# Two-layer GRU and mixture of experts on one core: at which slots of a chunk layer 1 makes all its gates in one PSUM bank

## The reference, cut to what matters

```python
def step(h, xt):
    hg = h @ Whh.T + bhh
    xr, xz, xn = jnp.split(xt, 3, axis=-1)
    hr, hz, hn = jnp.split(hg, 3, axis=-1)
    r = jax.nn.sigmoid(xr + hr)
    z = jax.nn.sigmoid(xz + hz)
    n = jnp.tanh(xn + r * hn)
    h_new = (1.0 - z) * n + z * h
...
h1 = _gru_layer(mixed, Wih0, Whh0, bih0, bhh0)
h2 = _gru_layer(h1, Wih1, Whh1, bih1, bhh1)
...
x = x + gated_output(h2)       # and then
x = x + mixture_of_experts(x)
```

## Time and profile before

| what | value |
|---|---|
| median of 3 runs | 2167.6 us (2160.2 to 2175.3) |
| the profiled execution's own time | 2176.5 us |
| its span, first to last instruction | 2174.5 us |
| slots, of which the last 19 hold layer 1 alone | 1043 |
| PE, DVE, ACT busy | 95%, 84%, 52% |

### The profile page before, as it was taken

How to read it: one execution, slowest core, us unless ns; L and a number is a source line. 1 busy time by engine, 2 the same in 40 slices (tenths; PEclk the granted TensorE clock), 3 DMA queues, 4 the chain that set the end, 5 groups by cost and what they waited for, 6 DMA issues and landing times.

```text
span 2174.5 us, 162405 instructions
## 1 busy us (share of the span) xinstructions
PE 2061.9 (95%) x70040; PEld 1501.8 (69%) x70040; DVE 1818.0 (84%) x11343; ACT 1141.1 (52%) x6471; POOL 560.3 (26%) x2542
## 2 busy tenths in 40 slices
PE   6999999999999999999999999999999999999997
PEld 4666667777677776777667776777767776777765
DVE  3788888888888888888888888888888888888885
ACT  2555555555555555555555555555555555555542
POOL 1222232222322223222232222222232222222220
PEclk9999999999999999999999999999999999999999
DMA  5000000000000000000000000000000000000000
GB/s 220 5 5 5 4 5 5 5 5 5 10 5 5 5 5 10 5 5 5 10 5 5 5 5 10 5 5 5 5 10 5 5 5 10 5 5 9 5 5 9
DMA packets 7184, 24.32 MB, mean 11 GB/s; under 512 B 1584, under 2 KB 3904, under 8 KB 6208
## 3 DMA queue, kind: packets, MB, share of 16 engines
q1 hardware_dynamic: 6464, 13.93, 1.7%
HBM read 11.83 MB, written 2.10 MB: 6 GB/s over the span
## 4 chain that ended last, share of the span: by engine, by line
PE 61%; DVE 25%; ACT 10%; issue 3%; DMA 0%; SPq 0%; POOL 0%; POOLq 0%; DVEq 0%
PE bank L335 28%; PE bank L327 18%; PE bank L267 11%; DVE bank L406 8%; DVE cells L426 7%; ACT factors L476 6%; DVE z_pre L407 5%; DVE r_pre L397 4%; ACT cells L480 4%; PE bank L308 3%; DVE bank L415 1%; PE bank L274 0%; DMA x_t<-in_x_t 0%; DVE x L682 0%; DVE n_second L382 0%
## 5 line engine op out<-in xcount | busy, mean ns | idle before, releaser
L335 PE MATMUL bank<-w_h,cells 128*22 128x128 f32 (+4 forms) x32768 | 1377.8, 281 | 22.8 <-DVE cells L426 11.9
L335 PEld LDWEIGHTS bank<-w_h,cells 128*22 128x22 f32 (+4 forms) x32768 | 865.7, 111 | 129.5 <-DVE cells L426 81.1
L327 PEld LDWEIGHTS bank<-w_h,cells 128*2 128x2 f32 (+15 forms) x28112 | 527.2, 113 | 493.8 <-DVE cells L426 464.8
L521 POOL TENSOR_SCALAR cells<-cells 128x4 f32<-128x4 f32 x2048 | 463.7, 226 | 1516.8 <-DVE cells L426 1515.1
L327 PE MATMUL bank<-w_h,cells 128*2 128x64 f32 (+15 forms) x28112 | 782.5, 225 | 72.8 <-DVE cells L426 54.0
L470 ACT ACTIVATE n_second<-r_pre 128x4 f32<-128x4 f32 x2048 | 426.5, 208 | 516.1 <-DVE r_pre L397 477.3
L476 ACT ACTIVATE factors<-z_pre 128x4 f32<-128x4 f32 x2048 | 429.5, 210 | 478.7 <-DVE z_pre L407 427.6
L426 DVE TENSOR_TENSOR_SCAN cells<-factors,cells 128x18 f32<-128x18 f32 x2048 | 396.5, 194 | 227.2 <-ACT cells L480 154.2
L406 DVE STREAM_TRANSPOSE bank<-bank 128x64 f32<-128x64 f32 x2048 | 520.6, 254 | 57.5 <-PE bank L335 36.2
L397 DVE STREAM_TRANSPOSE r_pre<-bank 128x64 f32<-128x64 f32 x2048 | 482.0, 235 | 36.4 <-PE bank L327 25.8
L407 DVE STREAM_TRANSPOSE z_pre<-bank 128x64 f32<-128x64 f32 x2048 | 429.2, 210 | 0.0
(11 more groups left out here) (90 smaller groups left out, 599.9 us busy)
## 6 DMA issues: line engine op xcount, KB each, us to landing
x_t<-in_x_t SPq DMA_DIRECT2D x4, 512.0 KB, 7.0
w_1e<-in_w_1e SPq DMA_DIRECT2D x1, 2048.0 KB
w_2e<-in_w_2e SPq DMA_DIRECT2D x1, 2048.0 KB
w_x<-in_w_x SPq DMA_DIRECT2D x2, 768.0 KB, 8.2
w_h<-in_w_h SPq DMA_DIRECT2D x2, 768.0 KB, 9.5
w<-in_w SPq DMA_DIRECT2D x3, 512.0 KB
out_y<-y SPq DMA_DIRECT2D x6, 256.0 KB, 2.5
w_in<-in_w_in SPq DMA_DIRECT2D x1, 256.0 KB, 2.5
```

What stands on the lines that cost most here:

```text
L327: mm = pe.matmul(r_sums[l][p][32 * g:32 * g + B * (j + 1)], state_tile(l, j, kt), w_h[l][:, kt, g, 2 * U:], start=False, stop=False, tile_ ...
L335: mm = pe.matmul(sums[l][p][32 * g:32 * g + B * (j + 1), 0:width], state_tile(l, j, kt), w_h[l][:, kt, g, 0:width], start=False, stop=Fals ...
L521: pool.tensor_scalar(cell_part(step_rows(l, j), 3), cell_part(step_rows(l, j), 1), 0.5, None, ALU.mult)\
```

## The change

Below slot 896, layer 1 makes its gates in one bank at places 0 and 8 in place of 4 and 12. Layer 0 keeps 4 and 12. From slot 896 on nothing changes. (The added line moves all later line numbers of the changed kernel by one: L335 becomes L336.)

```diff
@@ -20,6 +20,7 @@
 LAG = CH + 3
 SHORT = 56 * CH
+ONE_BANK = ((4, 12), (0, 8))
...
@@ -43,7 +44,7 @@
     s = t + LAG * l
-    return s % CH not in ((0, 4, 8, 12) if s >= SHORT else (4, 12))
+    return s % CH not in ((0, 4, 8, 12) if s >= SHORT else ONE_BANK[l])
```

## The result

| | before | after |
|---|---|---|
| median | 2167.6 us (2159.3 to 2175.3, 19 runs) | 2176.1 us (2171.1 to 2182.4, 19 runs) |
| span of the profiled execution | 2174.5 us | 2179.9 us |

The ratio is 1.0042 (95% interval 1.0031 to 1.0053): 8.5 us between the medians, 0.4% slower. The two profiled executions differ by only 5.4 us in their spans, because they start differently: slot 32 (the end of h0) is reached at 86.80 us before and at 83.66 after. All twelve traces of this case reach it between 83.46 and 87.23 us, with no relation to the table of one-bank places. From slot 32 on the changed kernel takes 8.5 us more, as the medians say.

A forecast was written before the change was run, and what follows sets the result against it. The prediction took layer 1's loop of waits to bound the kernel, with stalls where PE's instruction refill lags. Steps +22 us less 11 us of stalls gave +11 us, a median of 2179 us; range 2159 to 2193.

The forecast's parts named there:

- Place 8 and place 0: Layer 1 in one bank there: turn r waits for PE's end, nothing hides it, +0.22 us a slot each.
- Place 4: Layer 1 with r first there: the wait for PE goes, DVE's own chain binds, 2.13 to 2.10 us, -0.03.
- Place 12: Layer 1 with r first there: 0.03 to 0.04 us sooner, but layer 0's own loop binds behind it, counted 0.
- Sum of the clean slots: Step changes at all places without stalls: 0.41 us a chunk, 22 us in all.
- Stalls: Mixture's slots: PE's stream refills slower than busiest slots eat; stalls 0.87 to 0.64 us a chunk, 11 us back.
- Rival 1: Gaps in PE's stream are single late refills, not pace: whole 22 us appears, 2190, up to 2193; chance 0.22.
- Rival 2: Stalls at places 8 to 11 and 0 to 3 shrink more than steps grow: faster, 2160 us; chance 0.15.
- Rival 3: PE's supply or work binds, not layer 1's loop: only chunks without mixture pay, +3, 2171 us; chance 0.18.
- The Trainium skill's rule: Look first at the highest-occupancy engine: DVE's 84% against PE loads' 69%, DVE's work unchanged, so the time would stay.

The follow-up runs named there:

- e9: Kernel before, but DVE's turn r of layer 1 at places 0 and 8 waits for PE's last group; PE's instructions unchanged: 2181.4 us against 2170.1, ratio 1.0052.
- e1: Changed kernel with layer 1 never in one bank below slot 896: 2204.1 us against 2174.5 for the kernel before, ratio 1.0129.
- e5: Kernel before with each mixture and projection product cut into column halves, 8 matmuls where 4 stood: 2338.3 us, ratio 1.0737.
- e3: Kernel before with each mixture and projection product as one matmul of 128 stationary columns in place of four of 32: 2278.4 us, ratio 1.0472.
- e4: Changed kernel with one matmul of 128 stationary columns in place of four of 32 for mixture and projections: 2297.8 us, ratio 1.0560 to the kernel before.
- e2: Changed kernel with layer 1 in one bank at places 0, 4, 8 and 12 below slot 896: 2167.4 us against 2174.5 for the kernel before, ratio 0.9965.
- e7: Kernel before, but both layers in one bank at places 0, 4, 8 and 12 from slot 152 on: 2160.6 us against 2177.7, ratio 0.9920.
- e8: Kernel before, but layer 0 in one bank at places 0, 4, 8 and 12 below slot 896, layer 1 at 4 and 12: 2162.6 us, ratio 0.9934.
- e10: e7 with both layers making r first in every slot below 152: 2156.6 us against 2170.1 for the kernel before, ratio 0.9940.
- e6: Changed kernel with each mixture and projection product cut into column halves: 2341.9 us, ratio 1.0741 to the kernel before.

## Why the prediction was right, point by point

The forecast was +11 us on the median, made of 22 for the steps less 11 for stalls; 8.5 were measured. Both parts were there: by the profiled executions some 20 for the steps (0.39 us x 46 chunks and 0.3 x 8) less 12 for stalls.

- *Place 8 and place 0.* Forecast +0.22 us each. The clean slots go from 1.93 to 2.14 and from 1.95 to 2.16, +0.21 each, and e9, with +0.23 each, shows that the wait of turn r makes all of it.
- *Place 4.* Forecast -0.03, with nothing lost behind it. Place 4 does lose 0.03 (2.14 to 2.11), but place 5 gains 0.03 (1.93 to 1.96), and h0 to h0 there stays at 1.91. So behind place 4 too layer 0's own loop binds next, as I had it for place 12 alone. e1 says the same: with layer 1 r first at both places the clean chunk is 31.73 us against 31.67. This step failed; it was worth 1.7 us of the 22.
- *Place 12.* Forecast 0, measured -0.03 at 12 and +0.04 at 13: right.
- *Sum of the clean slots.* Forecast 0.41 us a chunk, measured 0.39 with the mixture. Without it the medians grow by 0.34, and the whole stretch by 0.29 a chunk (2.06 us over 7 chunks where 2.9 was forecast), since the kernel before had 0.07 us a chunk of stalls there too, and the changed one 0.03. In this stretch layer 0's loop was the longer one at places 5 to 11 (h1 ends 1.05 us after h0, the least that was seen), so layer 1 makes up 0.01 to 0.02 us of its delay at each of places 9 to 12, 14 and 15. The term was too large by 0.07 a chunk there, and the whole by 0.12, over 8 chunks 1 us.
- *Stalls.* Forecast 0.23 us a chunk back, from 0.71 to 0.34 at places 0 to 3 and 8 to 11 and from 0.16 to 0.30 at the others; measured 0.27 back, 0.75 to 0.28 and 0.15 to 0.35. The size and the places are as forecast, and the cause, a refill that comes late, is what the q8 packets show. But the size was partly luck. I had it from the spacing of the thin slots. e9 leaves those with few records where they were and gets back 0.28, as much within what one execution can tell. What counts for the sum, by this pair, is how much longer the chunk is and how many records it has, and the changed kernel has the same number; the spacing says at which places the stalls show. The working had two slips besides, which work against each other: 23 of 30 is three quarters and not two thirds, so that the 0.34 should be 0.29, and the 0.30 at the other places has no working behind it, where the same proportion, at 61 records a us, leaves 0.45. Done as it says, the sum is 0.74, 6 us come back and the net is +16: still inside the forecast's +5 to +18, but farther from what was measured.
- *Rival 1* (the whole 22 us, from single late refills and no pace) is ruled out by the result, whose interval ends at 11.5 us, and by e5, which has 232 gaps where the kernel before had 69, with only 29 more packets. Nearly the whole cost does appear between e3 and e4, 19 us, where there are few stalls to give back. It was right in one thing: each gap ends on a single refill. *Rival 2* (faster) is a true mechanism with too little to gain here; e2, e7, e8 and e10 decide for it because they also remove records. *Rival 3* (the pace is the bound, so the change costs nothing) is the case of e5 and e6. The kernel as it stands lies between the two: 19, 8.5 and 4 us (the last not clear of 0) for the same change as the load on PE's stream goes up.
- *The Trainium skill's rule* ("Perfetto Trace Analysis", Identifying the Most-Contended Engine) to look at the engine with the highest occupancy gave no change, since it points at DVE. The shares of the changed kernel stayed at 95%, 68% and 84%, and the time moved by 0.4% all the same. In e5 DVE's busy time is nearly unchanged too (1827.5 us against 1818.0) and the kernel takes 7% longer. In this case the measurement decides against the rule.

## What to carry to other kernels

Read a loop of waits slot by slot, with the median slot apart from the mean one. The medians tell what a step costs, the difference tells of stalls that have another cause, and a change can move the two against each other. Where an unrolled stream has gaps with no semaphore behind them, divide its records by the time of several stretches, and see whether the gaps end a fixed time after an instruction packet: if the quotient is the same wherever gaps appear, instructions are a resource, and fewer of them can be worth a longer critical path (e2, e7). Group work so that its result is ready early only for whoever can take it early: r first was worth 0.21 us at places 0 and 8 and next to nothing at 4 and 12, where turn r stood behind another long step.

## What the runs showed of the hardware that was not expected

PE took no more than 67 to 68 records a us, weight loads and matmuls together, over any long stretch of these twelve runs: 66.7 before, 66.5 after, 67.6 in e1, 66.9 and 67.1 in e5 and e6, 66.8 in e10's first stretch. Single slots run at 75 a us. At 64 B a record, 67 a us are 4.3 GB/s, in packets of 16 KB (8.98 MB in 548).

Where gaps are common, the q8 packets come at the same distance whatever the kernel: the median over the long stretch is 3.78 us before, 3.76 in e1, 3.77 in e5 and in e6, and 256 records in 3.77 us are 68 a us. In e7, which has 10 gaps in place of 69, it is 3.98. A gap in PE's loads ends some 1.4 us after the packet has ended (the middle half of the 69 gaps before: 1.35 to 1.46; of the 232 in e5: 1.34 to 1.48). So the gaps are waits for the refill of the instruction stream. What sets the distance of the packets stays open; no run changed the refill itself.

In slot 472 one fp32 matmul with 128 stationary and 256 moving columns (two records, 0.70 us from first start to last end) let the next weight load start 0.22 us after the state was there; behind four matmuls of 32 stationary columns (eight records, 0.61 us) it was 0.05.
